# Loops written out, first ranking spread over fifteen groups, and the last group's work and the second gather moved into the feed-forward

## The chip, the cores and the metric

One Trainium2 chip, one core. The metric is the device time of one execution in microseconds, lower is better. All times below are microseconds (us) unless ns is written. The trace is of one profiled execution; a position in it is given in us from the start of its span.

## The reference, cut to what matters

Eight batches (b) of 1024 tokens, 512 wide. Two blocks, each with layer norm, a scale and shift per batch from a small modulation matrix, and a gate:

```python
h = _layernorm(x) * (1 + ca) + sa
x = x + ga * attn(h)                    # q, k, v of shape (16 heads, 32, 1024), softmax over 1024
h = _layernorm(x) * (1 + cb) + sb
x = x + gb * ffn(h)
# ffn: scores = h @ w_router; the 512 best tokens of each batch go through
#      gelu(sel @ W1 + b1) @ W2 + b2, times sigmoid(score), added to h at their rows
```

The attention reshapes (1024, 512) straight to (16 heads, 32, 1024), so the work of four heads needs only 256 tokens. Those 256 tokens are a group (g), four to a batch, 32 in all.

## The kernel before

**Attention.** TensorE, ScalarE, VectorE and GpSimd each have a `body(b, last)` that does the four groups of a batch. For batches 0 to 6 it stands in a hardware loop (`Fori(0, B - 1)`, L528, L739, L918, L1201, L1488), with waits against registers; for batch 7 it is written out (`body(LAST, True)`). A group is 16 pairs (p) of units; a unit is one 128 x 1024 tile of scores in one of three PSUM slots. Per unit TensorE makes the scores (`scores_of`, L571), VectorE the negated row maximum (`row_max`, L1049), ScalarE the exponential (`exp_unit`, L845), which frees the slot. TensorE does things in program order: scores of a pair, the products of the pair four back (`products`, L620), and a third of a slice of the next group's keys, values or queries (L583, L595); after pair 9 also eight transposes of the group after next into a slot (`transposes`, L606). VectorE puts between its maxima the division by the sums (`q_over_sums`, L1092 and L1097, on even pairs), the gates (`gated`, L1074), layer norm statistics (`stats_of_x`, L977; `stats_of_x2`, L1079), and the router's dot products (`dot_router`, L1065). GpSimd is paced by those divisions (`behind_qn`, j = 0 to 7 at pairs 0, 2, ... 14). It splits keys and values in two float16 parts (`split_kv`, L1356 to L1360), adds the residual (`residual`, L1386) and does the second norm of the group before: `normed_before`, `h_times`, `h_plus` (L1395), `base_times` (L1395), `base_plus` (L1419, signals `post_done`). SyncE stores the result (`store_rows`, L449 and L450, eight DMAs) behind `post_done`.

**Ranking.** A token's rank is a count over the 1024 scores of its batch, in eight tiles of 128 tokens. `count_before(t)` (L88) compares with the t x 128 scores before the tile, `count_above(t)` (L95, L99) with the rest and counts ties. `find_slots` (L107 to L116) turns the ranks to slots, GpSimd writes them out with eight indirect DMAs (`store_kept`, L123), SyncE reads them back (`load_kept`, L479), and VectorE makes indices (`numbers`, L1129). GpSimd then gathers the rows of h (`gather_h`, L1434) and of the output (`gather_base`, L1440). Batch 0 is ranked on VectorE in groups 0 to 2 of batch 7 (`rank_first`), batch 1 in steps f = 0 to 4 of the first feed-forward pass (`count_tile`), batch n + 1 in steps 2 to 5 of pass n.

**Last group (batch 7, group 3).** TensorE has no next group to prepare. Between the units it transposes the gathered rows of batch 0 (`transpose_kept`, L684) behind pairs 6, 9, 12 and 14 (`KEPT_AT`). ScalarE and VectorE split the first weights (`high_part`, L878; `low_part`, L1124).

**Feed-forward.** Pass n (batch n) has 16 steps f: TensorE `ff1(n, f)` (12 matmuls, L758), then `ff2_of(n, f - 2)` (12 matmuls, L771), in one fixed order over the passes. ScalarE does the gelu (L935), VectorE splits it (L1259, L1261). In steps 12 to 15 of pass 0 TensorE transposes the gathered rows of batch 1, so `gather_h(1)` must have landed by step 12. `ff2_of(1, 0)` waits, in pass 1, for the split of step 0 and for `update_scaled(0, kt)` (L1243). `update_parts(0)` (L1230 to L1236) stands on VectorE at the end of step 15 of pass 0; it waits until every `store_rows` has landed, since its output buffers are those that are stored. GpSimd, at the start of the feed-forward: `residual(B, 0)`, `gather_base(0)`, `store_kept` of batch 1, second norm of the last group with its `base_plus`, then it waits until all stores have landed, then `gather_h(1)` and `gather_base(1)`.

## Time and profile before

| what | value |
|---|---|
| median of 3 runs | 2355.57 us (2354.59 to 4581.02) |
| the profiled execution | 2355.1 us |
| its span (first to last instruction) | 2353.4 us |
| mean granted TensorE clock | 0.991 |
| TensorE busy, share of the span | 2262.2 us, 96% |
| VectorE busy | 1907.9 us, 81% |
| ScalarE busy | 1486.8 us, 63% |
| GpSimd busy | 1240.0 us, 53% |

The span is the profiled execution's own; 1.7 us lie outside it. Busy TensorE time is modelled at its ends, so that 96% says only that few long gaps are left. The attention runs from 56 to 1651 us, the feed-forward from 1651 to the end.

### The profile page before, as it was taken

Reading aid. Unit: us, or ns where it says so; the run is one execution under the profiler, and the core shown is the slowest. Engines: PE = TensorE matmul, PEld = TensorE weight load, DVE = VectorE, ACT = ScalarE, POOL = GpSimd, SP = SyncE. Lnnn points to the kernel's source line nnn. Section 1 sums busy time; section 2 is a strip of 40 time slices with the busy share of each in tenths; the row PEclk is TensorE's granted clock in tenths of the full one; section 3 lists DMA queues with packets and bytes.
Section 4 is the critical chain, followed back from the end, with each engine's and each line's share of the span. In section 5 each row is a group of like instructions: output and inputs, shape, how many; then the busy total and the mean of one; then the engine's idle time right before and its main releaser. Section 6 shows DMA issues by size and latency. Waiting matters only on the chain.

```text
span 2353.4 us, 40956 instructions
## 1 busy us (share of the span) xinstructions
PE 2262.2 (96%) x12786; PEld 879.9 (37%) x12786; DVE 1907.9 (81%) x2909; ACT 1486.8 (63%) x2622; POOL 1240.0 (53%) x1117
## 2 busy tenths in 40 slices
PE   6999999999999999999999999887979999999998
PEld 3333333333333333333333333231434444444443
DVE  5999999999999999999999999998844653663543
ACT  2888888888888888888888887777311111111111
POOL 5667666677666766667766676554512222212300
PEclk9999999999999999999999999999989999999999
DMA  7333343333333334333333333223422011111100
GB/s 238 82 73 80 76 100 72 79 92 72 84 93 73 81 75 100 73 79 93 72 85 92 73 81 79 69 58 110 135 76 59 25 61 50 45 41 50 59 19 18
DMA packets 121371, 180.81 MB, mean 77 GB/s; under 512 B 43736, under 2 KB 43736, under 8 KB 120576
## 3 DMA queue, kind: packets, MB, share of 16 engines
q1 hardware_dynamic: 111152, 152.03, 26.4%
q0 software_dynamic: 9728, 25.23, 3.4%
q8 instruction: 117, 1.92, 0.3%
q14 instruction: 166, 1.36, 0.2%
q10 hardware_dynamic: 208, 0.28, 0.1%
HBM read 67.18 MB, written 43.16 MB: 47 GB/s over the span
## 4 chain that ended last, share of the span: by engine, by line
PE 67%; DVE 17%; issue 7%; POOL 4%; ACT 3%; DMA 1%; SPq 0%; DVEq 0%; POOLq 0%; ACTq 0%
PE sc L571 13%; PE acc L620 13%; PE sc L758 13%; PE sc L771 13%; DVE nmax L1049 11%; PE pj L583 7%; PE pj L595 6%; POOL x L1386 2%; ACT probs L845 1%; PE sc L606 1%; DVE stats L1079 1%; DVE qn L1097 1%; DVE x L1074 1%; POOL sel_rows L123 1%; DVE tie_out L99 1%
## 5 line engine op out<-in xcount | busy, mean ns | idle before, releaser
L845 ACT ACTIVATE probs<-sc,nmax 128x1024 f32<-128x1024 f32 x1024 | 1136.9, 1116 | 240.3 <-DVE nmax L1049 234.1
L1049 DVE TENSOR_REDUCE nmax<-sc 128x1 f32<-128x1024 f32 x1024 | 1218.9, 1214 | 52.3 <-PE sc L571 44.6
L620 PE MATMUL acc<-probs,qn 128*32 128x512 f32 x4136 | 552.1, 606 | 8.5 <-DVE x L1074 6.9
L583 PE MATMUL pj<-room 128*128 128x512 f16 x1500 | 386.5, 380 | 4.2 <-POOL room L1371 3.8
L935 ACT ACTIVATE probs<-sc,b_col 128x512 f32<-128x512 f32 x128 | 87.9, 687 | 470.9 <-PE sc L758 442.0
L771 PE MATMUL sc<-room,probs 128*128 128x512 f16 x1536 | 352.1, 379 | 0.0
L571 PE MATMUL sc<-stacks 128*128 128x512 f16 x1024 | 309.1, 384 | 19.1 <-ACT probs L845 17.6
L571 PE MATMUL sc<-room 128*128 128x512 f16 x1024 | 307.7, 382 | 20.3 <-ACT probs L845 9.4
L1259 DVE CAST probs<-probs 128x512 f16<-128x512 f32 x128 | 57.4, 448 | 256.0 <-ACT probs L935 217.9
L771 PEld LDWEIGHTS sc<-room,probs 128*128 128x128 f16 x1536 | 150.3, 98 | 181.2
L583 PEld LDWEIGHTS pj<-room 128*128 128x128 f16 x1500 | 144.6, 98 | 186.7 <-ACT room L816 13.2
L845 ACT ACTIVATION_READ_ACCUMULATOR probs<-sc,nmax 128x1 f32 x1024 | 206.1, 201 | 0.0
L595 PE MATMUL pj<-room 128*128 128x256 f16 x1512 | 188.0, 275 | 3.9 <-DVE room L1041 3.8
L1356 POOL TENSOR_TENSOR room<-room,k_bias 128x512 f32<-128x512 f32 x64 | 82.4, 1288 | 202.9 <-DVE qn L1097 116.0
L571 PEld LDWEIGHTS sc<-stacks 128*128 128x128 f16 x1024 | 74.9, 97 | 291.3 <-ACT probs L845 176.2
L571 PEld LDWEIGHTS sc<-room 128*128 128x128 f16 x1024 | 75.6, 97 | 289.1 <-ACT probs L845 175.5
L758 PE MATMUL sc<-stacks,room 128*128 128x512 f16 x768 | 176.2, 379 | 0.0
L620 PEld LDWEIGHTS acc<-probs,qn 128*32 128x32 f32 x4136 | 81.9, 108 | 230.2 <-issue 227.7
L595 PEld LDWEIGHTS pj<-room 128*128 128x128 f16 x1512 | 148.8, 99 | 49.7 <-issue 4.2
L1395 POOL TENSOR_TENSOR hbuf<-hbuf,rows 128x1024 f32<-128x1024 f32 x66 | 155.6, 2358 | 16.7 <-DVE qn L1097 16.4
L758 PE MATMUL sc<-qT,room 128*128 128x512 f16 x512 | 163.8, 382 | 0.1
L1360 POOL TENSOR_TENSOR room<-room 128x512 f16<-128x512 f32 x126 | 146.2, 1161 | 10.5
(164 smaller groups left out, 2236.9 us busy)
## 6 DMA issues: line engine op xcount, KB each, us to landing
stacks<-room SPq DMA_DIRECT2D x512, 64.0 KB, 2.0
room<-room SPq DMA_DIRECT2D x508, 64.0 KB, 2.0
h_rows<-hbuf SPq DMA_DIRECT2D x132, 128.0 KB, 2.3
out<-base SPq DMA_DIRECT2D x132, 128.0 KB, 2.6
room<-in_L_attn_x SPq DMA_DIRECT2D x96, 128.0 KB, 2.6
rows<-mod_rows SPq DMA_DIRECT2D x32, 256.0 KB, 4.1
room<-in_L_ffn_W SPq DMA_DIRECT2D x8, 1024.0 KB, 5.2
probs<-in_L_wmod SPq DMA_DIRECT2D x4, 1024.0 KB, 13.2
```

Of the source, the lines that this page charges most:

```text
L571: mm = nc.tensor.matmul(slot(g, v)[:, half * D:(half + 1) * D], stacks[g % 2][:, 0, hq, i * P:(i + 1) * P], stacks[g % 2][:, 1, hq, half * ...
L583: mm = nc.tensor.matmul(dst, hT16[par][:, a, cc, p * P:(p + 1) * P], w[:, z, cc, :], start=(t == 0), stop=(t == len(terms) - 1))
L595: mm = nc.tensor.matmul(dst[:, ci * 2 * P:(ci + 1) * 2 * P], wq16[:, z, cc, co * P:(co + 1) * P], hT16[par][:, a, cc, :], start=(t == 0), ...
L620: mm = nc.tensor.matmul(acc[at:at + DH, :], qn[:, (p // 2) % 2, p % 2, h2, :], probs[:, (2 * p + h2) % PROBS, half * D:(half + 1) * D], st ...
L758: mm = nc.tensor.matmul(ff[f % 2], w1_16[:, z, cc, f * P:(f + 1) * P], fT16[n % 2][a][:, cc, :], start=(t == 0), stop=(t == len(terms) - 1))
L771: mm = nc.tensor.matmul(ff2[kt], g16[:, nth(n, FC, f) % 3, a, kt * P:(kt + 1) * P], w2_16[:, z, f, :], start=(f == 0 and t == 0), stop=(f ...
L845: nc.scalar.activation(probs[:, u % PROBS, :], slot(g, ring_at(p, h2)), ACT.Exp, bias=nmax[:, u % PROBS:u % PROBS + 1], accum_out=rsum[:, ...
L935: nc.scalar.activation(g32[:, f % 2, :], ff[f % 2], ACT.Gelu_apprx_tanh, bias=b1_col[:, f:f + 1], scale=1.0 / WS).then_inc(gelu_done, 1)
L1049: nc.vector.tensor_reduce(nmax[:, u % PROBS:u % PROBS + 1], slot(g, ring_at(p, h2)), AX.X, ALU.max, negate=True).then_inc(max_done, 1)
L1356: nc.gpsimd.tensor_tensor(kv32[kk % 2][:], kv32[kk % 2][:], row, ALU.add).then_inc(kv_bias, 1)
L1360: nc.gpsimd.tensor_tensor(dst[:, 1], kv32[kk % 2][:], dst[:, 0], ALU.subtract).then_inc(kv_split, 1)
L1395: nc.gpsimd.tensor_tensor(dst, a, rows[:, row:row + 1, :].broadcast_to([P, SUBS, D]), op).then_inc(s_hm, 1)
```

## The change

1. **Loops written out.** All five `Fori` loops become Python loops, so batches 0 to 6 are straight code with constant waits.
2. **Ranking of batch 0.** `RANK_FROM` is 32 - 4 - 14 = 14. One counting step is done per group at pair 8, behind `q_over_sums`, in the fifteen groups 14 (batch 3, group 2) to 28 (batch 7, group 0). `weights` follows at pair 6 and `find_slots` at pair 8 of group 1 of batch 7. The scores are loaded at batch 3.
3. **The way from the slots to the transposes.** `store_kept` goes to the end of group 1 (two tiles) and the first pairs of group 2 (six tiles), `load_kept(0)` to group 2, `numbers(0)` to pair 14 of group 2, `gather_h(0)` before `behind_qn(1)` of group 3, and `load_weights(0)` to the start of group 2.
4. **Last group.** The second norm of the group before it (statistics, GpSimd's six operations, `dot_router`, `store_rows`) leaves group 3 and is done in pass 0 of the feed-forward: statistics at f = 5, dots at f = 10. That of the last group follows: statistics at f = 9, dots at f = 13, and the exponential of the scores at f = 14.
5. **Second gather.** GpSimd does `store_kept` of batch 1, norm, `h_times`, `h_plus` of group 30, then `gather_h(1)` at once, and only then the other base operations, the whole second norm of group 31 and `gather_base(1)`. The gathers read only the rows of batches 0 to n + 1, so they need not wait for the last stores. `numbers(1)` moves from f = 10 to f = 8. `load_kept(1)` stands before `load_weights(7)`, as it did.

```diff
+        RANK_FROM = NG - 4 - (2 * TB - 2)
@@ sync
-                    if last and g == 0:
-                        sp.wait_ge(s_sc, 16 * (B - 1))
+                    if b == RANK_FROM // GB and g == 0:
+                        sp.wait_ge(s_sc, 16 * b)
                         load_scores(0)
-                    if last and g == GB - 1:
-                        load_kept(0)
+                    if last and g == GB - 2:
                         sp.wait_ge(t_pe, NG)
                         load_weights(0)
+                    if last and g == GB - 1:
                         sp.wait_ge(r.s_slot, 1)
...
                         replicate((g + 1) % 2, 0, b * GB * 4 + 4 * (g + 1) + 2)
+                        if last and g == GB - 2:
+                            load_kept(0)
...
-            with sp.Fori(0, B - 1) as b:
+            for b in range(B - 1):
                 body(b, False)
             body(LAST, True)
...
+            load_kept(1)
+            load_weights(7)
             for n in ORDER:
-                if n + 1 < B:
-                    load_kept(n + 1)
                 if n == 0:
-                    load_weights(7)
+                    sp.wait_ge(post_done, NG)
+                    store_rows(NG - 2, (NG - 2) % 2)
                     sp.wait_ge(post_done, NG + 1)
                     store_rows(NG - 1, (NG - 1) % 2)
                     sp.wait_ge(s_dot, 2 * NG + 3)
                     store_scores(B - 1)
                     sp.wait_ge(s_sc, 16 * (B + 1))
+                elif n + 1 < B:
+                    load_kept(n + 1)
@@ scalar
-                    if n == 0 and f == 10:
+                    if n == 0 and f == 14:
                         act.wait_ge(s_dot, 2 * NG + 3)
@@ vector
+            def rank_first(n):
+                if n == 0:
                     nc.vector.tensor_copy(r.s8[:], scores[:, AHEAD:AHEAD + TB]).then_inc(s_s8, 1)
...
+                if n % 2 == 1:
+                    count_before(nc, dve, r, (n + 1) // 2, only)
+                else:
+                    count_above(nc, dve, r, n // 2, only)
...
-                        if end and p == 2:
+                        if last and g == GB - 2 and p == 14:
                             numbers(0)
...
                         if p == 11:
+                            if end:
+                                dve.wait_ge(post_done, NG - 1)
                             gated(b, g, 0)
...
-                        if p == 5 or p == 7:
+                        if (p == 5 or p == 7) and not end:
                             stats_of_x2(b, g, (p - 5) // 2)
-                        if p == 7:
+                        if p == 7 and not end:
                             aggregate2(b, g)
...
-                        if p == 15:
+                        if p == 15 and not end:
                             dve.wait_ge(s_hm, b * (3 * GB) + 3 * g + 2)
                             dot_router(0, b, g)
-                        if last:
-                            rank_first(g, p)
+                        if p == 8 and 0 <= b * GB + g - RANK_FROM < 2 * TB - 1:
+                            rank_first(b * GB + g - RANK_FROM)
+                        if last and g == 1 and p == 6:
+                            weights(slice(0, LAST * TB), 1)
+                        if last and g == 1 and p == 8:
+                            dve.wait_ge(s_tok, 3)
+                            find_slots(nc, dve, r, r.tokens[:, 0:TB, :], only)
...
             gated(B, -1, 1)
-            dot_router(1, B, -1)
...
                         if f == 5:
                             for s in range(SUBS):
+                                stats_of_x2(LAST, GB - 1, s)
+                            aggregate2(LAST, GB - 1)
+                        if f == 9:
+                            dve.wait_ge(s_xh2, NG)
+                            for s in range(SUBS):
                                 stats_of_x2(B, 0, s)
                             aggregate2(B, 0)
...
-                        if f == 9:
+                        if f == 10:
+                            dve.wait_ge(s_hm, LAST * (3 * GB) + 3 * (GB - 1) + 2)
+                            for s in range(SUBS):
+                                dot_router(s, LAST, GB - 1)
+                        if f == 13:
                             dve.wait_ge(s_hm, B * (3 * GB) + 2)
                             for s in range(SUBS):
                                 dot_router(s, B, 0)
-                        if f == 10:
+                        if f == 8:
                             numbers(1)
-                        if f == 12:
+                        if f == FC - 1:
                             weights(slice(LAST * TB, B * TB), 2)
@@ gpsimd
+                    if end:
+                        break
                     behind_qn(b, g, 3)
...
-            residual(B, 0)
             wait_alone(pv_done, ALL_PAIRS)
             gather_base(0, out_rows[0:T])
+            residual(B, 0)
             wait_alone(r.s_slot, 2)
             store_kept(nc, r, sel_rows, range(TB))
+            normed_before(LAST, GB - 1)
+            h_times(LAST, GB - 1)
+            h_plus(LAST, GB - 1)
+            gather_h(1, h_rows[0:2 * T])
+            base_times(LAST, GB - 1)
+            base_plus(LAST, GB - 1)
             normed_before(B, 0)
             h_times(B, 0)
             h_plus(B, 0)
             base_times(B, 0)
             base_plus(B, 0)
+            gather_base(1, out_rows[0:2 * T])
...
-                if n + 1 < B:
-                    if n:
-                        wait_alone(r.s_slot, n + 2)
-                        store_kept(nc, r, sel_rows, range(TB))
-                    else:
+                if n and n + 1 < B:
+                    wait_alone(r.s_slot, n + 2)
+                    store_kept(nc, r, sel_rows, range(TB))
+                    if n == B - 2:
                         for i in range(2):
                             pool.wait_ge(s_st[i], 128 * (NG // 2 + i) + 16)
-                    gather_h(n + 1, h_rows)
-                    gather_base((n + 1) % 2, out_rows)
+                    gather_h(n + 1, h_rows[0:(n + 2) * T])
+                    gather_base((n + 1) % 2, out_rows[0:(n + 2) * T])
```

## Rows read from the trace of the kernel before

**Rows 1.** Busy time by stretch: us, PE, PEld, DVE, ACT, POOL busy (x), PEclk, DMA share, GB/s.

```profile
250.97:1230.82 979.85, 970.05 (x5924) 349.20 (x5920) 933.03 (x1241) 847.72 (x1525) 656.79 (x580) 1.00 0.35 82
1230.82:1425.22 194.40, 193.89 (x1188) 69.96 (x1190) 186.51 (x249) 168.12 (x303) 131.40 (x116) 1.00 0.35 82
1425.22:1480.52 55.30, 50.16 (x306) 17.57 (x304) 53.60 (x82) 42.34 (x78) 32.87 (x29) 1.00 0.35 84
1480.52:1538.70 58.18, 50.08 (x298) 16.89 (x296) 56.53 (x87) 42.28 (x78) 32.97 (x29) 1.00 0.30 71
1538.70:1592.09 53.39, 48.63 (x290) 16.18 (x288) 50.93 (x71) 41.90 (x75) 31.33 (x27) 1.00 0.24 53
1592.09:1650.79 58.70, 41.41 (x231) 9.07 (x230) 51.06 (x69) 45.25 (x74) 24.17 (x18) 0.91 0.39 116
```

**Rows 2.** The same view, six pairs of a looped and of a straight group.

```profile
1279.26:1297.12 17.86, 17.86 (x104) 5.09 (x101) 17.11 (x24) 15.67 (x29) 8.52 (x9) 1.00 0.47 119
1425.22:1442.99 17.77, 17.77 (x104) 5.19 (x102) 16.95 (x24) 15.64 (x29) 8.50 (x9) 1.00 0.48 116
```

**Rows 3.** Timeline at a loop's back edge: start, us, engine, line, op, tiles, shape, [idle before].

```profile
447.08 1.23 DVE L1049 TENSOR_REDUCE nmax<-sc 128x1 f32<-128x1024 f32 x1 [1.80 <-PE sc L571]
```

**Rows 4.** Timeline of pairs 9 and 10 in a looped group (batch 6, group 1).

```profile
1305.76 2.34 DVE L1049 TENSOR_REDUCE nmax<-sc 128x1 f32<-128x1024 f32 x2
...
1306.44 1.26 POOL L1356 TENSOR_TENSOR room<-room,v_bias 128x512 f32<-128x512 f32 x1
...
1307.08 1.12 ACT L845 ACTIVATE probs<-sc,nmax 128x1024 f32<-128x1024 f32 x1
...
1307.21 1.09 PE L606 MATMUL sc<-ident,room 128*128 128x128 f32 x8
...
1308.34 0.61 PE L571 MATMUL sc<-stacks 128*128 128x512 f16 x2
```

**Rows 5.** Groups of VectorE's instructions, 1425 to 1592 us: count | busy, mean ns | idle before.

```profile
L99 DVE SCALAR_TENSOR_TENSOR tie_out<-srow,s,earlier 128x128 bf16<-128x128 f32 x8 | 10.7, 1334 | 0.0
...
L95 DVE TENSOR_SCALAR_CACHE_REDUCE cmp_out<-srow,s 128x1024 bf16<-128x1024 f32 (+7 forms) x8 | 6.4, 802 | 0.0
...
L88 DVE TENSOR_SCALAR_CACHE_REDUCE cmp_out<-srow,s 128x128 bf16<-128x128 f32 (+6 forms) x7 | 5.2, 738 | 0.0
```

**Rows 6.** Timeline of the second tile's ties in batch 7, group 0, with GpSimd's operation.

```profile
1460.02 2.35 POOL L1395 TENSOR_TENSOR hbuf<-hbuf,rows 128x1024 f32<-128x1024 f32 x1 [0.42 <-DVE qn L1097]
...
1460.83 1.69 DVE L99 SCALAR_TENSOR_TENSOR tie_out<-srow,s,earlier 128x128 bf16<-128x128 f32 x1
```

**Rows 7.** Chain that ended last, first ties in the feed-forward: start, us, what.

```profile
1656.97 0.27 DVE tie_out L99 x2
```

**Rows 8.** Timeline of VectorE in the last group, pair 2.

```profile
1601.78 0.17 DVE L1129 CAST kept_i<-kept 128x4 int32<-128x4 f32 x1 [2.92 <-DMA kept<-sel_rows]
```

**Rows 9.** Busy time by stretch: pass 0 and pass 1 of the feed-forward.

```profile
1650.72:1747.49 96.77, 82.17 (x380) 37.84 (x377) 57.91 (x109) 25.62 (x29) 40.64 (x30) 0.91 0.39 116
1747.49:1832.12 84.63, 84.63 (x403) 39.45 (x400) 45.81 (x109) 13.98 (x21) 19.92 (x20) 1.00 0.16 47
```

**Rows 10.** Timeline of TensorE where pass 0 stops.

```profile
1727.81 1.11 PE L684 MATMUL pj<-ident,stacks 128*128 128x128 f32 x4 [14.49 <-DMA stacks<-h_rows,kept_i]
```

**Rows 11.** Chain that ended last, from the last norm to that stop.

```profile
1701.64 4.29 POOL base L1419
...
1709.25 9.63 DMA out<-base
...
1723.63 4.13 DMA stacks<-h_rows,kept_i
```

**Rows 12.** Timeline of GpSimd and of VectorE between passes 0 and 1.

```profile
1693.96 4.84 POOL L1395 TENSOR_TENSOR hbuf<-hbuf,rows 128x1024 f32<-128x1024 f32 x2
...
1748.93 0.68 DVE L1230 TENSOR_TENSOR gb_b<-probs 128x512 f32<-128x512 f32 x1
...
1751.11 2.74 DVE L1236 SCALAR_TENSOR_TENSOR probs<-gb_b,kept,probs 128x512 f32<-128x512 f32 x4
```

More of the change, by code:

```diff
@@ L518, in body @@
                         replicate((g + 1) % 2, 0, b * GB * 4 + 4 * (g + 1) + 2)
+                        if last and g == GB - 2:
+                            load_kept(0)
                         replicate((g + 1) % 2, 1, b * GB * 4 + 4 * (g + 1) + 4)
-                    sp.wait_ge(post_done, b * GB + g + 1)
-                    store_rows(before[g], (g + 1) % 2)
+                    if not (last and g == GB - 1):
+                        sp.wait_ge(post_done, b * GB + g + 1)
+                        store_rows(before[g], (g + 1) % 2)
                     if g == 0:
@@ L737, in body @@
                             transposes(slot(g, T_AT))
-            with pe.Fori(0, B - 1) as b:
+            for b in range(B - 1):
                 body(b, False)
@@ L916, in body @@
                             evac_t(slot(g, T_AT), b * GB + g + 3).then_inc(slot_free, 1)
-            with act.Fori(0, B - 1) as b:
+            for b in range(B - 1):
                 body(b, False)
@@ L1199, in body @@
                             kept_low(0, CC - 1, aux[0])
-            with dve.Fori(0, B - 1) as b:
+            for b in range(B - 1):
                 body(b, False)
@@ L1454, in body @@
                         normed_x((g + 2) % 4, n3)
-                    behind_qn(b, g, 1)
+                    if last and g == GB - 2:
+                        store_kept(nc, r, sel_rows, range(2, 4))
                     if end:
                         gather_h(0, h_rows[0:T])
-                    else:
-                        split_kv(nxt, 0, n4 + 1, n4 + -1)
+                    behind_qn(b, g, 1)
+                    if not end:
+                        split_kv(nxt, 0, n4 + 1, n4 + 1 - 2)
+                    if last and g == GB - 2:
+                        store_kept(nc, r, sel_rows, range(4, 6))
                     behind_qn(b, g, 2)
                     residual(b, g)
+                    if last and g == GB - 2:
+                        store_kept(nc, r, sel_rows, range(6, TB))
+                    if end:
+                        break
                     behind_qn(b, g, 3)
-                    if not end:
-                        split_kv(nxt, 1, n4 + 2, n4 + 0)
+                    split_kv(nxt, 1, n4 + 2, n4 + 2 - 2)
                     normed_before(b, g)
-                    if last and g == GB - 2:
-                        wait_alone(r.s_slot, 1)
-                        store_kept(nc, r, sel_rows, range(0, TB // 4))
                     behind_qn(b, g, 4)
-                    if not end:
-                        split_kv(nxt, 2, n4 + 3, n4 + 1)
+                    split_kv(nxt, 2, n4 + 3, n4 + 3 - 2)
                     h_times(b, g)
@@ L1474, in body @@
                     h_plus(b, g)
-                    if not end:
-                        split_kv(nxt, 3, n4 + 4, n4 + 2)
+                    split_kv(nxt, 3, n4 + 4, n4 + 4 - 2)
                     behind_qn(b, g, 6)
```

30 lines of the change are left out of this document (4 added, 26 removed).

## The prediction

> **What bounds the kernel now.** I read the mean clock, then busy time by group of the attention, then the chain of waits and the timelines where a stretch is longer than its neighbours. Busy shares alone say nothing here: TensorE is always "busy". Three things are to be seen.
>
> Looped batches are even. Five of them take 979.85, so 195.97 each; batch 6, whose last group runs on into straight code, takes 194.40, or 48.6 a group, of which TensorE is busy 48.5 and VectorE 46.6 [rows 1]. TensorE sets the pace. The rest of those 196 is the back edge, where VectorE stands 1.80 for TensorE's first scores [rows 3].
>
> Batch 7 is not even: 55.30, 58.18, 53.39, 58.70 against 48.6 [rows 1]. In its first three groups VectorE's busy time grows by 7.0, 9.9 and 4.3 over 46.6, and the time by 6.7, 9.6 and 4.8: nearly all ranking there is paid.
>
> Pass 0 of the feed-forward takes 96.77, pass 1 84.63 [rows 9]. Pass 0 has two blocks of 12 matmuls fewer (steps 0 and 1 have no second layer): a block is (84.63 - four times 0.44 of transposes)/32 = 2.59, so pass 0 should take 79.45. It loses 17.3. TensorE stands 14.49 before the first transpose of batch 1 [rows 10]; the granted clock is 0.91 in the mean of the pass and 1.00 in pass 1 [rows 9], and the rest is work at 1.2 instead of 2.4 GHz behind that stop. The chain behind it is the base work of the last group, the landing of its stores, then the gather [rows 11].
>
> **The change part by part**, against the profiled span of 2353.4; the execution was 2355.1, so 1.7 lie outside, and the median of the runs shown is 2355.57, 0.5 above it.
>
> 1. *Back edges.* Six are taken. Each batch loses 195.97 - 194.40 = 1.57 [rows 1]; the group after an edge begins with all slots free and is some 0.12 shorter (48.28 to 48.45 against the 48.57 that I take without an edge: my estimate from the starts of the groups), so 1.45 is net. **-8.7**, between -6 and -11.
>
> 2. *Constant waits.* Six pairs of a looped group take 17.86, the same six of straight group 28 17.77 [rows 2]: 0.09 in six pairs. Over 27 groups that is 2.4 if only these pairs gain. TensorE's own order hides the register work, so I take no more. **-2.4**, between 0 and -6.
>
> 3. *Ranking steps.* VectorE has 2 a group to spare on paper [rows 1], and a step of 1.1 would vanish in it, if place did not matter. It does. The step stands behind pair 8's division, so it delays the maximum of pair 9, which began at 1305.76. That maximum's exponential starts at 1307.08 and ends at 1308.20; the scores of pair 10, which need its slot, start at 1308.34 [rows 4]. 0.14 is what such a release takes wherever TensorE is seen waiting in batch 7, so the slack is zero, and TensorE has none elsewhere to win it back. I take each step as fully paid.
>  The steps' own size: seven `count_before` 5.2, eight comparisons of `count_above` 6.4 [rows 5], eight ties. An undisturbed tie is 0.27 (first in the feed-forward) [rows 7]; in batch 7 the mean was 1.334 [rows 5], because a tie that meets a GpSimd tensor operation stands until that ends: 1.69, from 1460.83 to 1462.52, with GpSimd's ending at 1462.37 [rows 6]. At pair 8 GpSimd starts a `split_kv` addition 0.68 after the place of the step and ends it at 1.94 [rows 4]. The comparisons fall from about 1.28 for 1024 scores to 0.34 for 128 (mean 0.802). Tiles 0 to 3 compare longer than 0.68, so their ties end at 1.94 + 0.15: 2.09 each, 8.4 together. Tile 4 is on the edge, 1.5. Tiles 5 to 7 come through ahead: 0.8, 0.67 and 0.54. Sum 11.9, with 5.2 it is 17.1, of which 0.5 falls into batch 7. **+16.6** in groups 14 to 27; below 0 (all hidden), above 21.5 (every tie blocked at 2.1).
>  The Trainium skill, page "SBUF — State Buffer", section "Who interferes with whom", says that a VectorE instruction with two SBUF inputs contends with GpSimd instructions that read SBUF, that the first one holds the port for its whole length, and that a float32 copy within SBUF may contend too. The ties agree (1.69). By that rule the copy of the scores at the head of the first step, which falls on `normed_before`'s last operation, could lose as well and push that step from 2.1 to 3.7, the sum by 1.6; no row shows it, and the sum here leaves it out.
>
> 4. *Batch 7.* Group 0: 48.6 and the last tile's 0.5, 49.1; -6.2. Group 1: `weights` 0.75 at pair 6, then `find_slots`, about 1.0 of six small operations that meet the same addition, so 2.3: 51.6; -6.6. Bounds 49.5 and 53. Group 2: no ranking and no eight transposes (1.09) [rows 4]; six indirect DMAs of 1.3 come on GpSimd, which is busy 31 of 53 here and where they stand behind divisions 6 apart; 47.5; -5.9. `numbers(0)` at pair 14 comes some 15 after the last `store_kept`, so I expect no wait. Group 3: VectorE is the bound (51.06 busy of 58.70, the end included [rows 1]). It loses the wait of 2.92 and its conversion [rows 8], two statistics and the aggregate (1.5), and about half of what the late weights cost ScalarE at pair 4. The dot behind the last maximum lies beside the last exponential and gives nothing. Some 1.1 more from shorter stalls at pairs 9 and 10: 52.7; -6.0. Sum **-24.7**, between -20 and -29. The new wait on `post_done` at pair 11 is for work that ended a group earlier.
>
> 5. *Pass 0.* `gather_h(1)` now follows `h_plus`, which ended at 1698.80 [rows 12] and ends there again, since ranking, `store_kept` and the norm ahead of it are the same work. Four gathers at 1.25: the last starts at 1702.6 and lands 4.13 later [rows 11], 1706.8. TensorE wants it 14.5 before 1727.8, at 1713.3. It has 6.5 to spare, so the whole 17.3 goes. **-17.3**.
>  What is late next: GpSimd's remaining list grows by four gathers (5.0) and one whole norm (3.5 and four operations of 2.4) ahead of the last `base_plus`. From 1698.8: gathers to 1703.9, base of group 30 to 1709, with 2.3 for VectorE's two-input work between 1711.4; norm 3.5, four operations 9.7, 1.4 of such blocking: 1726. In the old trace the last `base_plus` ended at 1705.93 and the last store landed at 1718.88, 13.0 later [rows 11]. So stores land at 1739. `update_parts(0)` waits for that and takes 4.9, from 1748.93 to 1753.85 [rows 12]: 1744. Behind it VectorE does the splits of steps 0 and 1 (1.1 each) and the first `update_scaled` (0.6): 1746.8. Pass 1 begins at 1650.72 + 79.45 = 1730.2, and five blocks of 2.59 on, at 1743.1, TensorE needs exactly these for `ff2_of(1, 0)`. New wait 3.7, and 0.8 for a lowered clock: **+4.5**, between 0 (landing in 3, not 10) and 13 (GpSimd 5 later, clock down for longer).
>
> Sum: 2353.4 - 8.7 - 2.4 + 16.6 - 24.7 - 17.3 + 4.5 = 2321.4; with 1.7 outside, **2323**, 1.4% below 2355.57.
>
> **The rivals.**
> A. *The ranking steps hide.* For: VectorE's 2 a group [rows 1]. Against: zero slack at just that slot [rows 4], and batch 7, where nothing was hidden. It takes 16.6 and the 0.5 off: 2306.
> B. *The stop moves instead of going.* The list on GpSimd, or the landing of the last stores, is later than worked out, `update_parts(0)` holds VectorE longer, and TensorE stands 15 at `ff2_of(1, 0)`, with its clock down. For: POOL's operation stretched to 4.29 from 2.4 and stores landed after 9.63 [rows 11]. Against: the work on GpSimd's list is nearly all known. 2323 + 11 = 2334.
> C. *Slower: straight code must be fetched.* 28 groups now run once each. Were TensorE to stand once a group for its next stretch of code as at the edge (1.45), that is 28 x 1.45 = 40.6 and the 8.7 not won on top of it: 2323 + 8.7 + 40.6 = 2372. It decides from 1.2 a group ((2355 - 2323)/28) on. Against: group 28 is straight already and no slower in six pairs [rows 2].
> D. *The last groups don't gain.* ScalarE and TensorE turn out to hold group 3 and group 1 where they are, half of the 24.7 stays: 2335.
>
> **How the numbers follow.** The forecast 0.64, A 0.12, B 0.12, C 0.03, D 0.09. Forecast's own terms: edges 2, constants 3, steps 5, batch 7 4, pass 0 5, together some 9 either way. With A and B cut at a tenth each side the range is 2306 to 2337. A measurement here tells about 2% from no change, 47 us, so faster than 2308.5: most of A and a little of the forecast's tail, 0.13. Slower by 2% is C alone, 0.02. The rest, 0.85, is within 2%.
>
> **What would show it.** Looped batches at 194.3 without ranking; groups 14 to 27 alternately longer by about 2.1 (ties of tiles 0 to 3) and by 0.3 to 1.1 (comparisons before), the delay always at the scores of pair 10. Batch 7 at about 201. `gather_h(1)` landed before 1713 on the old count from the start of the feed-forward, no wait at the first transpose, and a wait of some 4 at L771 in step 2 of pass 1, released by VectorE behind L1230 to L1236. Wrong would be: groups 14 to 27 at 48.6 (A); a TensorE wait over 8 in pass 1 or a renewed wait at L684 (B); "issue" waits of TensorE spread over all batches (C); group 3 of batch 7 over 56 (D).

## The result, and the profile after

| | before | after |
|---|---|---|
| median | 2355.54 us (4 runs) | 2327.25 us (2322.39 to 2328.77, 4 runs) |
| profiled execution | 2355.1 us | 2328.8 us |
| its span | 2353.4 us | 2327.0 us |
| mean granted TensorE clock | 0.991 | 0.992 |

The ratio is 0.9876, 95% interval 0.986 to 0.9892: 1.2% less time. That is clear of the noise, and within the 2% on either side that the prediction counted as no change. 2323 was forecast, 4 us away. One run of the kernel before (4581.02 us) and one of e_p15 below (4657.76) took twice as long as the others, and no ratio here uses them. The spans differ by 26.4 us. The first lines of the page (span; busy time, share and instructions of each engine):

```profile
span 2327.0 us, 35730 instructions
...
PE 2258.0 (97%) x12786; PEld 883.2 (38%) x12786; DVE 1903.7 (82%) x2909; ACT 1490.0 (64%) x2622; POOL 1244.4 (53%) x1117
```

Every engine has as much to do as before; what went is waiting. Cut at the same places as [rows 1, 9], the kernel after reads so (us, then PE, PEld, DVE, ACT, POOL busy, PEclk, DMA share, GB/s). The lines are the first fourteen groups, which have no ranking, the fourteen with a ranking step each, batch 7 group by group, and passes 0 and 1:

```profile
52.91:731.62 678.71, 675.00 (x4124) 244.88 (x4128) 652.63 (x871) 592.60 (x1065) 459.51 (x406) 1.00 0.35 82
731.62:1429.62 698.00, 681.01 (x4148) 246.17 (x4149) 663.30 (x912) 595.02 (x1070) 459.59 (x406) 1.00 0.34 79
1429.62:1478.98 49.36, 48.48 (x300) 17.46 (x302) 47.00 (x69) 42.54 (x78) 32.86 (x29) 1.00 0.34 82
1478.98:1531.60 52.62, 49.77 (x300) 17.62 (x302) 48.02 (x67) 42.88 (x79) 33.28 (x30) 0.97 0.32 76
1531.60:1580.18 48.58, 47.35 (x292) 16.69 (x294) 45.19 (x62) 40.72 (x74) 34.69 (x30) 1.00 0.47 86
1580.18:1634.90 54.72, 41.89 (x238) 9.30 (x236) 49.02 (x62) 46.42 (x76) 6.70 (x5) 0.94 0.30 92
1634.90:1716.30 81.40, 79.62 (x381) 37.02 (x378) 66.72 (x113) 25.52 (x29) 54.03 (x37) 1.00 0.38 113
1716.30:1805.83 89.53, 86.25 (x402) 39.71 (x400) 46.45 (x112) 13.98 (x21) 22.54 (x23) 0.98 0.26 75
```

678.71 over 14 groups is 48.48 a group, the pace of TensorE. Against the old trace the differences are:

| stretch | change | forecast |
|---|---|---|
| up to the first row maximum | -2.7 | 0 |
| groups 0 to 13 (three back edges gone) | -5.5 | -5.6 |
| groups 14 to 27 (three edges gone, 14 steps added) | +12.6 | +11.1 |
| batch 7 | -20.2 | -24.7 |
| pass 0 | -15.4 | -17.3 |
| pass 1 and what follows | +4.8 | +4.5 |

(In the forecast's column the 8.7 of the edges and the 2.4 of the waits are split evenly over the 28 groups that were looped.) So batch 7 and pass 0 gave up 35.6, and 12.6 of it came back in groups 14 to 27. The start-up's 2.7 is no gain of the change: the first row maximum stands between 52.4 and 55.1 in the twelve traces of the changed kernel and its variants. The first group varies with it: it takes 47.7 in six of the twelve, the four latest starts among them, and 48.7 to 49.0 in the other six. It took 47.8 before and 48.7 after, so the 5.5 of groups 0 to 13 is too small a gain: the six traces with 47.7 need 677.7 to 678.0 for them, 6.1 to 6.4 less than before.

**A ranking step.** The timeline of group 14, from the division of pair 8 to the scores of pair 10 (the lines that bear on it):

```profile
757.75 0.29 DVE L1105 TENSOR_TENSOR qn<-qT,rinv 128x128 f32<-128x128 f32 x1
757.95 0.17 DVE L1148 COPY s<-scores 128x8 f32<-128x8 f32 x1
...
758.15 1.28 DVE L95 TENSOR_SCALAR_CACHE_REDUCE cmp_out<-srow,s 128x1024 bf16<-128x1024 f32 x1
...
758.65 1.27 POOL L1365 TENSOR_TENSOR room<-room,v_bias 128x512 f32<-128x512 f32 x1
...
759.36 0.71 DVE L99 SCALAR_TENSOR_TENSOR tie_out<-srow,s,earlier 128x128 bf16<-128x128 f32 x1
...
760.00 2.34 DVE L1057 TENSOR_REDUCE nmax<-sc 128x1 f32<-128x1024 f32 x2
...
762.51 0.69 PE L579 MATMUL sc<-room 128*128 128x512 f16 x2 [1.98 <-ACT probs L853]
...
763.13 1.94 PE L628 MATMUL acc<-probs,qn 128*32 128x512 f32 x8
```

Read it down: comparison, then a tie that ends only with GpSimd's addition (758.65 + 1.27 = 759.92), then the two maxima, one exponential, and TensorE, which has stood 1.98 for the slot. Pair 8 is 4.69 to 4.70 long in the groups of tiles 0 to 4, where it is 2.65 without a step, and the step is 2.04 to 2.05 long: it is paid in full, as the prediction had it, and at the place that it named. The last line is the new thing: eight matmuls took 1.94 here, 1.07 at the same place of the next trace (a_again). Over the 4 us from there the granted clock was 0.57:

```profile
762.50:766.50 4.00, 3.99 (x14) 0.88 (x15) 2.10 (x3) 3.97 (x8) 1.79 (x1) 0.57 0.39 88
```

**Pass 0.** The 14.49 wait of [rows 10] is gone; TensorE stands at one place only, for 1.78 in step f = 3, where the first tie of batch 1's ranking meets a GpSimd operation:

```profile
1640.56 2.37 POOL L1395 TENSOR_TENSOR x<-x,xt 128x1024 f32<-128x1024 f32 x1
...
1640.96 2.13 DVE L99 SCALAR_TENSOR_TENSOR tie_out<-srow,s,earlier 128x128 bf16<-128x128 f32 x1
```

That is `residual(B, 0)`, which the change put behind `gather_base(0)`. The tie, 0.27 in [rows 7], took 2.13, and the step, from its first matmul to the next step's, took 7.12; it took 5.45 before, and a step without a wait takes 5.18.

**Pass 1.** The forecast's new wait is there. The chain that ended last (start, us, what), and TensorE's timeline behind it:

```profile
1717.90 6.92 DMA out<-base
...
1725.51 1.67 DVE hbuf L1232 x4
1727.18 2.65 DVE probs L1236 x4
```

```profile
1732.69 4.22 PE L779 MATMUL sc<-room,probs 128*128 128x512 f16 x12 [3.28 <-DVE hbuf L1243]
```

In order: the last store, `update_parts(0)`, then the splits and `update_scaled` (not shown), and a block of 12 matmuls in 4.22 instead of 2.59. The stop is 3.28 where 3.7 was forecast, and the lowered clock costs 1.6 where 0.8 was.

### The profile page after: what moved, and what is told of

The parts are those of the page before. It is cut to its first block, busy times and chain, and to the rows that moved or that the text cites. A ratio compares the mean times of both kernels' runs of the same rounds, so it can differ in the third digit from the quotient of the medians.

```text
span 2327.0 us, 35730 instructions
## 1 busy us (share of the span) xinstructions
PE 2258.0 (97%) x12786; PEld 883.2 (38%) x12786; DVE 1903.7 (82%) x2909; ACT 1490.0 (64%) x2622; POOL 1244.4 (53%) x1117
## 4 chain that ended last, share of the span: by engine, by line
PE 68%; DVE 21%; POOL 5%; ACT 3%; issue 2%; DMA 1%; SPq 0%; POOLq 0%; DVEq 0%; ACTq 0%
DVE nmax L1057 15%; PE acc L628 14%; PE sc L579 14%; PE sc L779 12%; PE sc L766 12%; PE pj L603 7%; PE pj L591 7%; POOL x L1395 2%; ACT probs L853 2%; DVE stats L1087 1%; DVE qn L1105 1%; DVE dot_out L1073 1%; PE sc L614 1%; ACT room L831 1%; DVE x L1082 1%
## 5 line engine op out<-in xcount | busy, mean ns | idle before, releaser
L1057 DVE TENSOR_REDUCE nmax<-sc 128x1 f32<-128x1024 f32 x1024 | 1217.5, 1213 | 51.4 <-PE sc L579 47.6
```

The lines of the kernel that those rows point to most:

```text
L1057: nc.vector.tensor_reduce(nmax[:, u % PROBS:u % PROBS + 1], slot(g, ring_at(p, h2)), AX.X, ALU.max, negate=True).then_inc(max_done, 1)
```

## The experiments

Each is the kernel after with one edit, unless it says otherwise. A ratio is to the kernel before on the same chip, with its 95% interval. The variants ran on three chips: a_again, e_p15, e_loops and e_resid on one, e_gbase, e_scores, e_dense and e_gath on another, e_noties, best1 and best2 on the third. Most readings are by stretch of the trace, because the executions of the kernel after scatter by 6 us (of that more below). The third step of pass 1 is f = 2.

| kernel | median | groups 14 to 27 | batch 7 | pass 0 | third step of pass 1 |
|---|---|---|---|---|---|
| after, first trace | 2327.25 | 698.0 | 205.3 | 81.4 | 10.1 |
| a_again | 2330.37 | 696.8 | 205.1 | 81.4 | 13.2 |
| e_p15 | 2317.70 | 685.8 | 204.0 | 81.4 | 11.3 |
| e_loops | 2335.79 | 699.8 | 204.7 | 81.4 | 13.8 |
| e_resid | 2325.53 | 696.8 | 204.9 | 79.7 | 8.4 |
| e_gbase | 2322.35 | 697.1 | 203.7 | 81.4 | 5.2 |
| e_scores | 2325.27 | 698.3 | 203.7 | 81.4 | 7.4 |
| e_dense | 2325.87 | 697.1 | 204.0 | 81.4 | 7.2 |
| e_gath | 2344.23 | 696.7 | 205.1 | 103.0 | 5.2 |
| e_noties | 2319.04 | 689.6 | 202.9 | 81.4 | 7.0 |
| best1 | 2309.62 | 685.6 | 203.3 | 79.7 | 5.2 |
| best2 | 2305.62 | 685.7 | 200.6 | 79.7 | 5.2 |

What follows the third step of pass 1 takes 590.3 in all of them.

### The kernel after once more (a_again)

No edit.

> The changed kernel once more, unedited, as the yardstick for the kernels that run beside it. In the first profiled execution two of the five long ranking groups (14 and 20) had a stop of TensorE of 2 us followed by matmuls at half speed, 1.1 to 1.3 us each. If such drops come and go, the executions spread over some 2320 to 2330, median near 2326, and another trace shows them in other groups, or not at all. If they belong to the place in the program, the same two groups show them again.

Measured: 2330.37 (2329.35 to 2330.76), ratio 0.9893 (0.9878 to 0.9907). All five stops of 1.98 are at their places again, but the clock fell behind one alone, and not one of the two of the first trace: group 14 took 50.68 (51.89 in the first trace), group 20 50.43 (51.93), group 22 51.94 (50.67). At the place quoted above the matmuls now run at full speed:

```profile
762.28 0.60 PE L579 MATMUL sc<-room 128*128 128x512 f16 x2 [1.98 <-ACT probs L853]
762.82 1.07 PE L628 MATMUL acc<-probs,qn 128*32 128x512 f32 x8
```

So the drops come and go. The median was above the range that I gave by 0.4. The larger part of the scatter is pass 1, whose third step took 13.2 here and 10.1 there, a thing that I had not expected.

### Straight code and edges (e_loops)

```diff
-            for b in range(B - 1):
+            with pe.Fori(0, 3) as b:
                 body(b, False)
+            for b in range(3, B - 1):
+                body(b, False)
```

The same on all five engines.

> Batches 0 to 2 stand in hardware loops again, batches 3 to 7 in straight code. By the prediction's terms three back edges of 1.45 come back, 4.4 us, and the waits against registers 12 x 0.09 = 1.1: together 4.4 to 5.5 more than the changed kernel. If the start-up's 2.7 us (first row maximum at 52.91 instead of 55.64) also comes from the entry to the loops, it comes back too, and the sum is 7 to 8; if it has another cause, the first row maximum stays near 52.9. Rival (straight code costs as much as it saves, the edges being replaced by fetching): no difference.

Measured: 2335.79, ratio 0.9916 (0.9903 to 0.9929), 5.4 above a_again; from the first row maximum to group 12 it took 587.1 against 582.2 (a_again) and 582.0 (after): 4.9 to 5.1. I had miscounted: a loop of three batches goes back twice, not three times. The two groups with an edge at their end take 50.34 and 50.29 instead of 48.3 and 48.4, with the same wait of VectorE as [rows 3]:

```profile
249.61 2.58 DVE L1063 TENSOR_REDUCE nmax<-sc 128x1 f32<-128x1024 f32 x2 [1.75 <-PE sc L581]
```

An edge is thus 1.9 to 2.0, 3.9 for two, and the other 1.0 to 1.2 lies in small pieces of 0.1 to 0.25 in most of the groups. Loops cost what the theory says and a little more (4.0 by its terms for two edges and twelve groups); the first row maximum stayed at 52.90, so the start-up is not the loops' doing. Straight code costs nothing that shows, 28 groups long.

### Density of the steps (e_dense)

```diff
-                        if p == 8 and 0 <= b * GB + g - RANK_FROM < 2 * TB - 1:
-                            rank_first(b * GB + g - RANK_FROM)
+                        if b == LAST - 1:
+                            for k in DENSE.get((g, p), ()):
+                                rank_first(k)
```

`DENSE` puts steps 0 to 14 behind the even pairs from pair 6 of group 24 to pair 2 of group 26.

> The fifteen steps stand behind every second pair of groups 24 to 26, as densely as in the kernel before, instead of one a group in groups 14 to 28; weights and slots stay where the change put them. My theory: a step is paid at full size wherever it stands behind a division, so that spreading them bought nothing by itself: 24 to 26 grow by 17 to 22 together, groups 14 to 23 fall back to 48.5, and the total is within 3 us of the unedited changed kernel (2327 to 2332). Rival (density is what costs, a single step is cheaper than one among others): 5 to 10 us slower, 2335 or more.

Measured: 2325.87, ratio 0.9882 (0.9866 to 0.9899), the same as the kernel after within the intervals. Groups 24 to 26 take 55.51, 58.42 and 49.57, groups 14 to 23 48.52 in the mean. 163.50 less three times 48.52 is 17.9 for the fifteen steps:

```profile
1217.43:1380.93 163.50, 149.65 (x892) 51.93 (x894) 158.07 (x234) 127.03 (x231) 98.29 (x87) 0.99 0.31 75
```

With the same 48.52 the spread steps cost 698.0 - 14 x 48.52 = 18.7 in the first trace and 17.5 in the second, clock drops included. Spreading bought nothing by itself. A step is not cheap because it is alone: it is paid because its place has next to no slack. The two sets of steps are not of one size: some ties meet longer operations of GpSimd in e_dense, and its fifteen steps are 20.6 long together, against 17.3 in the kernel after. So packed steps were paid to nine tenths, spread ones in full.

### The same steps at another pair (e_p15)

```diff
-                        if p == 8 and 0 <= b * GB + g - RANK_FROM < 2 * TB - 1:
+                        if p == 15 and 0 <= b * GB + g - RANK_FROM < 2 * TB - 1:
```

> The fifteen ranking steps stand at the end of pair 15 instead of pair 8, where GpSimd's last operations of the group are over and the next group's are not yet begun. My theory (a step costs what the place has no slack for: zero behind pair 8, about 1 us behind pair 15, and ties cost 0.27 instead of 0.7 to 1.4): the steps are mostly hidden, groups 14 to 27 give back 15 to 17 us, about 2310. Rival (VectorE's work is paid wherever it stands, since TensorE never catches up): only the ties' blocking of 5 to 6 goes, about 2321. Second rival (place does not matter at all): 2327.

Measured: 2317.70, ratio 0.9839 (0.9826 to 0.9851), 12.7 below a_again; groups 14 to 27 in 685.8, 11.0 less. The tie of tile 0 takes 0.35 here, with no GpSimd operation beside it:

```profile
781.38 0.16 DVE L1148 COPY s<-scores 128x8 f32<-128x8 f32 x1
781.58 1.28 DVE L95 TENSOR_SCALAR_CACHE_REDUCE cmp_out<-srow,s 128x1024 bf16<-128x1024 f32 x1
...
782.78 0.35 DVE L99 SCALAR_TENSOR_TENSOR tie_out<-srow,s,earlier 128x128 bf16<-128x128 f32 x1
...
783.05 2.35 DVE L1057 TENSOR_REDUCE nmax<-sc 128x1 f32<-128x1024 f32 x2
```

Steps of `count_before` up to three tiles vanish (48.25 to 48.39 a group), those of `count_above` cost 0.3 to 1.7. In all 685.8 - 679.3 = 6.5 are still paid: my 15 to 17 was too much, because the slack behind pair 15 is 0.4 and not 1. The fourteen steps are 12.4 long together here, so 5.9 is hidden, 0.42 a step; the steps of 0.67, 0.80, 0.93 and 1.07 of `count_before` lengthen their groups by 0.3, 0.4, 0.5 and 0.65 over the 48.4 of such a group without a step. The 11.0 is then some 1.3 for the clock drop of a_again, 4 for ties that GpSimd no longer holds up, and 5.9 of slack. Without the drop it is 9.7, against 5.9 for leaving out the ties altogether (next), so both rivals fall. TensorE has no stop over 0.95 in these groups, and no clock drop.

### Steps without ties (e_noties)

```diff
+    if not ties:
+        nc.vector.memset(r.ties[:, t:t + 1], 0.0).then_inc(r.s_cmp, 1)
+        return
...
-                    count_above(nc, dve, r, n // 2, only)
+                    count_above(nc, dve, r, n // 2, only, False)
```

It leaves out the eight counts of equal scores of batch 0; a constant zero stands for them.

> Leaves out the eight counts of equal scores of batch 0 (a constant zero is written in their place), steps stay behind pair 8. What is left of a step is its comparison: 1.28, 1.14, 1.01, 0.87 and 0.74 instead of 2.04 in the first five, and 0.3 less in the last three, together 5.2 + 0.8 = 6.0. My theory adds that the drops of the clock come from stops of TensorE of about 2 us, so groups 14 to 22 show none with stops of 1.3 and less: 1.2 for each drop that the unedited kernel had (one or two), 7 to 8.5 in all, 2319 to 2323. Rival (the clock drops at places of its own): drops of 1.2 stay in one or two of these groups.

Measured: 2319.04 (2314.75 to 2324.8), ratio 0.9846 (0.9831 to 0.9861). Groups 14 to 27 take 689.6, 7.2 less than in a_again: 1.3 for the one drop of that trace, and 5.9 for the ties, where 6.0 was expected. The stop in group 14 is 1.35, and the matmuls behind it are at full speed:

```profile
761.78 0.60 PE L582 MATMUL sc<-room 128*128 128x512 f16 x2 [1.35 <-ACT probs L856]
762.32 1.06 PE L631 MATMUL acc<-probs,qn 128*32 128x512 f32 x8
```

### The residual's place (e_resid)

```diff
+            residual(B, 0)
             wait_alone(pv_done, ALL_PAIRS)
             gather_base(0, out_rows[0:T])
-            residual(B, 0)
```

> GpSimd's last residual stands before the wait and the gather of the output rows of batch 0 again, as before the change. My theory: in pass 0 the first tie of batch 1's ranking took 2.13 us because it met that residual, and TensorE's third step took 7.12 instead of 5.18; that goes, the step is 5.2 to 5.3 and pass 0 79.5 to 80 instead of 81.4; in all 1.5 to 2 us less. Rival: the first tie meets some other operation of GpSimd (store_kept, the norm), and the step stays near 7; no difference.

Measured: 2325.53, ratio 0.9878 (0.9863 to 0.9892). By the median 4.8 below a_again, of which the edit can claim 1.7: pass 0 in 79.68, its step f = 3 in 5.41 instead of 7.15. The tie is undisturbed, since GpSimd is issuing gathers then:

```profile
1640.60 0.35 DVE L99 SCALAR_TENSOR_TENSOR tie_out<-srow,s,earlier 128x128 bf16<-128x128 f32 x1
```

The rest is the third step of pass 1, 8.4 instead of 13.2, which scatters anyway. The prediction's 79.45 for a pass 0 without waits is met to 0.23, and the edit's theory holds.

### The gather of h back (e_gath)

```diff
             h_plus(LAST, GB - 1)
-            gather_h(1, h_rows[0:2 * T])
             base_times(LAST, GB - 1)
...
             base_plus(B, 0)
+            gather_h(1, h_rows[0:2 * T])
             gather_base(1, out_rows[0:2 * T])
```

> The second gather of h goes behind the last base operation again, with no wait on the stores. It is then issued at 79.5 after the start of the feed-forward instead of about 51, and lands at 87 to 88, while TensorE wants it at about 64. My theory: TensorE stops 23 to 24 us in pass 0, its clock falls and costs 1 to 3 more; the wait in pass 1 (5 to 8 us with its clock) is swallowed. Net 17 to 21 us slower than the unedited kernel, about 2347. Rival (moving the gather was not what removed the stop of pass 0, the shorter wait on stores was): under 5 us slower.

Measured: 2344.23, ratio 0.9955 (0.9938 to 0.9971), 13.9 to 17 above the kernel after. Pass 0 takes 103.0 (+21.6), TensorE stands 19.14, and pass 1's wait is gone (-4.9 to -8.0):

```profile
1707.33 1.10 POOL L1443 DMA_INDIRECT stacks<-h_rows,kept_i  x1 [0.17 <-issue]
```

```profile
1716.93 1.12 PE L692 MATMUL pj<-ident,stacks 128*128 128x128 f32 x4 [19.14 <-DMA stacks<-h_rows,kept_i]
```

The stop is 4 to 5 below my 23 to 24. GpSimd's last base operation ended 73.6 after the start of the feed-forward and not 79.3, because the gathers ahead of it had gone; I had forgotten that they take GpSimd's time too. The rival falls: with no wait on the stores, but the gather late, the stop is all there. And it shows the bargain of the change's two last parts: with the norm of group 30 moved here, pass 0 would be 6 longer than it was (103.0 against 96.8 [rows 9], 1.7 of it the residual's place) had the gather not been moved ahead of it.

### What holds the last stores (e_gbase, e_scores)

```diff
             base_plus(B, 0)
+            for i in range(2):
+                pool.wait_ge(s_st[i], 128 * (NG // 2 + i) + 16)
             gather_base(1, out_rows[0:2 * T])
```

> The gather of the output rows of batch 1 (4 transfers of 256 KB that now start beside the last stores) waits until all stores have landed. My theory: the wait in pass 1 is as long as it is because the last four stores share the DMA engines with that gather; in the unedited kernel they were issued at 79.7 to 83.4 after the start of the feed-forward and VectorE went on at 90.0 to 92.1. Without it they land 3 us after the last issue, like the stores of the group before (2.2 to 2.7), and VectorE goes on at 86.5 to 87.5: TensorE's step in pass 1 shrinks from 10 to 13 us to 5.2 to 7, 4 to 6 us less in all, about 2325. Rival (the 4-byte pieces of the score transfer hold the engines): VectorE goes on no earlier than 89, gain under 1.5.

```diff
                     sp.wait_ge(s_dot, 2 * NG + 3)
+                    for i in range(2):
+                        sp.wait_ge(s_st[i], 128 * (NG // 2 + i) + 16)
                     store_scores(B - 1)
```

> SyncE writes the scores of the last batch only after all stores have landed. The rival to the theory on the gather: the score transfer (4 KB in 4-byte pieces, landed 9.2 to 9.9 after its issue) holds the last stores up. If so, the stores land at 86 to 87 after the start of the feed-forward and the step in pass 1 shrinks by 4 to 6 us, while the scores come 3 us later, at 97 to 98, and nothing waits for them in that time. If the gather of 1 MB is what holds them, VectorE still goes on at 89 or later, and the gain is under 1.5.

Measured: e_gbase 2322.35 (2320.72 to 2322.97), ratio 0.986 (0.9843 to 0.9876); e_scores 2325.27, ratio 0.9876 (0.9859 to 0.9892). The timelines of GpSimd and VectorE, first of a_again, where the gather runs beside the stores (issued from 1712.90 to 1716.64):

```profile
1712.68 1.08 POOL L1449 DMA_INDIRECT probs<-out,kept_i  x1 [0.17 <-issue]
...
1716.85 0.95 POOL L1449 DMA_INDIRECT probs<-out,kept_i  x1 [0.30 <-issue]
```

```profile
1725.39 0.69 DVE L1230 TENSOR_TENSOR gb_b<-probs 128x512 f32<-128x512 f32 x1 [9.17 <-DMA out<-base]
```

and of e_gbase (stores issued from 1713.01 to 1716.57):

```profile
1720.32 1.34 POOL L1449 DMA_INDIRECT probs<-out,kept_i  x1 [7.69 <-DMA out<-base]
```

```profile
1719.61 0.69 DVE L1230 TENSOR_TENSOR gb_b<-probs 128x512 f32<-128x512 f32 x1 [3.27 <-DMA out<-base]
```

From the end of the last base operation to VectorE's L1230 it took 6.8 to 7.0 us in the three traces with the gather held back (e_gbase, best1, best2) and 9.1 to 13.9 in the seven that leave the two transfers as they were. TensorE's third step of pass 1 was 5.18 in all three: no stop. With the score transfer held back it took 9.1, the low end of the others, so that run speaks neither for nor against a small part of it; the transfer alone is not the cause. By the medians e_gbase is 2.9 below e_scores and 3.5 below e_dense, which ran beside it. So the gather beside the stores makes the stop; that both use the DMA engines is the explanation that fits, and no run separates it from others.

### Together (best1, best2)

best1 has the edits of e_p15, e_resid and e_gbase; best2 also this one:

```diff
-                        if last and g == 1 and p == 8:
+                        if last and g == 1 and p == 15:
                             dve.wait_ge(s_tok, 3)
                             find_slots(nc, dve, r, r.tokens[:, 0:TB, :], only)
```

> Three edits at once: ranking steps behind pair 15, the residual ahead of the first gather in the feed-forward, and the second gather of output rows after the stores. Each took its part from a different wait, so they should add: the kernel with steps at pair 15 (2317.7) less 1.7 for the third step of pass 0 and 6.1 for pass 1 (its step of 11.25 back to 5.18): 2310. If they get in each other's way (the step of pass 1 above 5.2, or the third step of pass 0 above 5.5), 2313 or more.

> The same with the search for the slots behind pair 15 instead of pair 8 of group 1 of batch 7. In the trace of the kernel with steps at pair 15 that pair took 5.07 instead of 2.65 (and pair 10 took 4.47 instead of 3.26, at the lower clock behind the stop). Behind pair 15 there is about 1 us of slack and no operation of GpSimd to meet, so 1.5 to 3 less than best1, about 2308. Rival: GpSimd, which waits for the slots to send the first two tiles, falls behind in group 2 and gives it back there: no difference.

Measured: best1 2309.62 (2307.06 to 2310.16), ratio 0.9798 (0.9785 to 0.9812); best2 2305.62 (2305.17 to 2307.92), ratio 0.9785 (0.9771 to 0.9798). The edits add up, as each works on another wait: 2310 was expected of best1, and its third step of pass 1 is 5.2 and its pass 0 79.7. best2 is 4.0 below best1 by the medians, where 1.5 to 3 was expected; batch 7 accounts for 2.7 of it. In best2 group 1 of batch 7 takes 49.62 with the clock at 1.00, where it took 52.62 at 0.97, and group 2 gave nothing back (48.08):

```profile
1466.12:1515.74 49.62, 49.08 (x301) 17.50 (x298) 46.77 (x69) 43.07 (x78) 32.91 (x29) 1.00 0.34 82
```

best2 is 2.15% faster than the kernel before, and its executions lie within 2.8 us of each other.

## Why the prediction was right

The total was 4 off, and nearly every term was found at its place. That it was no more than 4 is in part luck. The terms together came to -23.7 where -32.0 was forecast, 8.3 less; 2.7 of that was made up by the earlier start, which no term names and which is not of the change, and 1.5 by the median, which lies that much below the traced execution. Part by part:

1. *Back edges*, -8.7. Two edges cost 3.9 in e_loops where 1.45 each was forecast. The stretch of groups 0 to 13, with three edges gone, gained 5.5, and 6.1 to 6.4 where first groups of one length are compared, where 5.6 was forecast together with the next term. Right in kind, and about 1 too small.
2. *Constant waits*, -2.4: 1.0 to 1.2 for twelve groups in e_loops, where 1.1 follows from the forecast. Right.
3. *Ranking steps*, +16.6. Without the clock drops the two traces say 18.7 - 1.2 - 1.5 = 16.0 and 17.5 - 1.3 = 16.2. Pair by pair: 2.04 for tiles 0 to 3 (2.09 forecast), 2.04 for tile 4 (1.5), 1.05 and 0.79 for tiles 5 and 6 (0.8 and 0.67). Right, zero slack included; what was missing is 1.2 to 1.5 for each clock drop behind a stop of 2 us. The Trainium skill, page "SBUF — State Buffer", section "Who interferes with whom", would by my reading of it have made the copy at the head of the first step wait and that step 3.7; the copy took 0.17 beside GpSimd's L1350, and pair 8 took the same 4.69 as without a copy. The 51.89 of group 14 is the clock, not the copy.
4. *Batch 7*, -24.7, measured -20.2. This is the term that was mis-sized most. Group 0 49.36 (49.1): right. Group 1 52.62 (51.6): `find_slots` cost 2.4 where 2.3 was forecast, but it stops TensorE for 2.37, and behind that the clock falls in seven traces (52.6 to 52.9) and not in e_gbase, e_scores and e_noties (51.4), nor in best1 (51.0). In best2 the group takes 49.62. Group 2 48.58 (47.5): the eight transposes taken away gave nothing, because TensorE then stands for the same time in their place:

```profile
1560.77 0.60 PE L579 MATMUL sc<-room 128*128 128x512 f16 x2 [1.16 <-ACT probs L853]
```

 I took 1.09 off TensorE's time in a place where VectorE and ScalarE were just as late. Group 3 54.7 (52.7): pair 2 lost 3.08 as forecast and pair 7 1.0, but pair 6 grew from 2.67 to 3.52. That again is the clock, behind a stop of 1.84:

```profile
1594.28 0.60 PE L579 MATMUL sc<-stacks 128*128 128x512 f16 x2 [1.84 <-ACT probs L853]
```

```profile
1595.50:1599.50 4.00, 4.00 (x17) 0.70 (x14) 3.01 (x3) 3.22 (x6) 1.81 (x1) 0.57 0.14 28
```

 The same stop is there in a_again, with the clock at 1.00 behind it, pair 6 at 2.67 and the group at 54.3. Against the kernel before, two things are then left: pair 0 takes 3.08 instead of 2.67, and pairs 9 and 10, where 1.1 was to be saved, take 3.58 and 4.39 instead of 3.58 and 4.07. Why they do, no run was made to find out; it stays open.
5. *Pass 0*, -17.3, measured -15.4: the stop went, and 1.7 of the missing 1.9 came from a term that I did not have, the residual in the way of a tie (e_resid). The gather landed about 2 before it was needed, not 6.5: in a_again, whose trace has the landing, at 1695.24, and the first transpose began at 1697.41. Its first piece was issued 50.8 after the start of the feed-forward, not 48.1, and its four pieces took 8.8 instead of 5.0 to issue, since two of them stood beside VectorE's `low_part` (below); TensorE came 1.5 later to the transposes. Right with less margin than I thought.
 *The new wait*, +4.5, measured +4.9 in the first trace and 8.0 in the second. Place and releaser were right, and the size in the first trace; 8.0 is well above 4.5 and inside the bounds of 0 to 13. Its cause was only half named: I carried over 13 us from the last base operation to the landing as a fact of the stores, and by e_gbase and the two best kernels 2 to 7 of the 9 to 14 that it takes in the other traces are due to the 1 MB of `gather_base(1)` beside them.

Of the rivals, A (steps hide) fell at pair 8 and is half true at pair 15, where 5.9 of 12.4 is hidden. B (the stop moves) happened in small: between 1.6 and 6.7 of stop in pass 1 in the kernels that leave the two transfers alone. C (fetching) has no sign in any trace. D (last groups don't gain) is a part of the truth, 4.5 of the 12 that it priced, some 1.2 and 0.4 of that for the clock in groups 1 and 3.

## What to carry to other kernels

Work added to an engine that is not the bound is paid or hidden by the slack of its place, not by the engine's spare time over the group: the fifteen steps cost 17.9 packed; fourteen of them cost 16 to 19 spread behind a division with no slack, and 6.5 spread behind pair 15 with 0.4 us of slack each and no GpSimd operation to meet. Before spreading work, find the pair with the most slack, and look there for what GpSimd is doing: a tie of 0.35 took up to 1.45 beside its addition. And when a transfer is moved forward, look at what else is then on the DMA engines: a gather of 1 MB that nobody waits for cost 2 to 9 us, since it ran beside four stores that everyone waited for.

## What the runs showed of the hardware that was not expected

**A stop of 2 us sometimes costs the clock.** In seven traces with five stops of TensorE of 1.97 to 1.99 us each (one 2.27) at the same places, the group was 1.2 to 1.5 us longer (once 1.9) behind 11 of 35, with no pattern that I see, and with the granted clock at 0.57 over 4 us where it was 1.00 in another trace. The same happened behind the stop of 2.37 of `find_slots` in 7 of 11 traces, and behind that of 1.84 in group 3 of batch 7 in 2 of 12 (the first trace and best1). Behind the stops of 1.35 and 1.02 in the ranking groups of e_noties it did not happen. In pass 1 stops of 1.62, 1.85, 2.09 and 3.06 lengthened the step by 0.16 more than themselves; those of 3.28, 4.22, 5.38 and 6.7 cost 1.6 to 2.6 on top, the block behind the 5.38 running all at 0.50, the lower level of 1.2 GHz:

```profile
1733.19:1738.20 5.01, 5.01 (x12) 1.72 (x13) 4.97 (x9) 0.00 (x0) 1.61 (x2) 0.50 0.04 13
```

So a stop of about 2 us can cost more than its length, in one execution and not in the next.

**GpSimd's gathers wait for VectorE.** The second and third piece of `gather_h(1)` took 2.89 and 2.94, against 0.94 for the fourth and 0.95 in e_gath, and each ended 0.8 after a `low_part` (1686.92 to 1689.18, 1690.16 to 1692.44). It is so in all eleven traces with the gather at this place; in e_gath, where no `low_part` runs beside the pieces, they take 0.94 to 0.96. GpSimd's and VectorE's timelines:

```profile
1687.13 2.89 POOL L1443 DMA_INDIRECT stacks<-h_rows,kept_i  x1 [0.30 <-issue]
1690.32 2.94 POOL L1443 DMA_INDIRECT stacks<-h_rows,kept_i  x1 [0.30 <-issue]
```

```profile
1686.92 2.26 DVE L1132 SCALAR_TENSOR_TENSOR room<-room 128x2048 f16<-128x2048 f32 x1
...
1690.16 2.28 DVE L1132 SCALAR_TENSOR_TENSOR room<-room 128x2048 f16<-128x2048 f32 x1
```

The same page and section of the Trainium skill, "SBUF — State Buffer", "Who interferes with whom", says that a VectorE operation with two inputs in SBUF contends with GpSimd's reads, and infers for `tensor_tensor` that the generation of descriptors is not held up by it. `low_part` is a `scalar_tensor_tensor` with two tensors in SBUF, and here the issuing of the gather was held up for as long as it ran. Whether the scatter of the stores' landing, 9.1 to 13.9 us with the gather beside them, has its cause in the DMA engines' order or elsewhere, no run settled.
